# Moving the output LayerNorm of a two-layer graph-attention block from VectorE to GpSimd

## The chip, the cores and the metric

The kernel runs on one core of a Trainium2 chip. The metric is the device time of one execution in microseconds (us), the median of three. TensorE is called PE in the rows, VectorE DVE, ScalarE ACT, GpSimd POOL and SyncE SP.

## The reference

x has shape (8, 1024, 256), adj is a 1024 x 1024 matrix of zeros and ones. Two residual stages follow each other, each on the clipped LayerNorm of x. The first mixes nodes with adj, the second is graph attention with four heads, then one head, then a feed-forward part, and a last LayerNorm with gain and offset:

```python
h = relu(layernorm(x)); x = x + (deg * (h Wi + b) + adj @ (h Wj))      # stage 1
h = relu(layernorm(x))
# stage 2, for each batch b, layer 1 with 4 heads, layer 2 with 1 head:
e = f1[:, None] + f2[None, :]; e = where(e > 0, e, 0.01 * e); e = where(adj > 0, e, -1e9)
h' = elu(softmax(e) @ (h W))
y  = relu(h' @ w1 + b1) @ w2 + b2 + h'
mu = mean(y); var = var(y)
x  = x + (y - mu) / sqrt(var + 1e-5) * ln_gamma + ln_beta              # the part that the change touches
```

## The kernel before

After a setup block, one long block runs a software pipeline over "units". A unit is one 128-row tile of attention for one head: layer 1 has 32 units a batch (8 tiles x 4 heads), layer 2 has 8, so 320 units in all. Every engine's program is written as one loop over a step number n, and at step n each engine does the work of a few units at fixed distances, in a fixed order. At step n:

- VectorE makes the masked row of unit n+5 (`masked_row`, L935, which also gives its maximum `mx`), then the low half of the probabilities of unit n+1 (`low_part`, L942). Every second step it does the ELU of a pair (L950, L955) and, in layer 1, `ht_lo` (L961).
- GpSimd works on one column a row tile: `inverse` of unit n+2 (L736, L738: one over the sum of the exponentials, `rden`), and at even n `shifts` for units n+4 and n+5 (L749, L751: from `mx` to the exponent's shift).
- ScalarE makes the leaky ReLU of unit n+4 (L804), the exponential of unit n+3 (L810, which needs `shift`), then `high_part` of unit n+2 (L817, p_hi, which needs `rden` and frees nothing until `low_part` has read it).
- SyncE transposes p_hi and p_lo by DMA into four slots, which TensorE frees when it has multiplied a pair; TensorE does a pair every second step.

`masked_row` of a unit waits for `low_part` five units before it, since five row buffers `xr` are there.

Around this run the other jobs, placed by a step number relative to a batch: `front` (the first stage of a batch three ahead: LayerNorm L996, h0 L1002, the bias L1008, `cat_low` L1015, products L1156) and, relative to the end of layer 2 of batch s (`at = n - end2[s]`), the feed-forward part of batch s in two halves i of four row tiles each. Half i goes: at 4i the first product, at 1 + 4i ScalarE's `hidden` (L875), at 2 + 4i the second product, at 3 + 4i VectorE's `y_out` (L1048 adds b2, L1051 and L1058 give mean and variance of four tiles in `mv_y`), at 4 + 4i GpSimd's `rsqrt` (L722, L724: `rstd_y`), at 5 + 4i VectorE's `gain` (L1066), at 6 + 4i VectorE's `rescale` (L1075), and at 7 + 4i and 8 + 4i GpSimd adds two row tiles each to the output in memory (`add_y`, L759, a DMA with accumulation). Both halves share `mv_y` and `rstd_y`, so `y_out` of the next half waits, ahead of L1058, until the last readers of the half before are through.

For batches 0 to 5 all of this lies inside the attention of the next batches; for batch 6 beside the last eight units; for batch 7 after everything else.

Of the kernel before, what the change touches and what calls it, by code (L numbers as in the profile page):

```python
# [29 lines left out]
def build(nc, x, adj, w0, b0, w_heads, a_heads, w_out, a_out, w1, b1, w2, b2, gamma, beta, out):  # L30
# [12 lines left out]
    with ExitStack() as ctx:  # L43
# [530 lines left out]
        lny_stats, lny_mv, lny_eps, lny_pow, lny_gain, lny_done = (sem(f"lny_{i}") for i in ("stats", "mv", "eps", "pow", "gain", "done"))  # L574
# [144 lines left out]
        def _(pool):  # L719
# [33 lines left out]
            def add_y(p, i, u):  # L753

                pool.wait_ge(lny_done, 2 * p + i + 1)
                pool.wait_ge(x1_saved, 4 * (p + 1) * DMA)
                tok = slice((4 * i + 2 * u) * P, (4 * i + 2 * u + 2) * P)
                to = out[p:p + 1, tok, :].rearrange("b (t p) f -> p (b t) f", p=P)
                pool.dma_start(to, y_half[i][:, 2 * u * F:2 * (u + 1) * F].rearrange("p (t f) -> p t f", f=F), accum_op=ALU.add).then_inc(out_added[i], DMA)  # L759

# [5 lines left out]
            for n in range(START, STOP):  # L766
# [5 lines left out]
                for s in range(B):  # L772
# [11 lines left out]
                    for i in range(2):  # L784
                        if at == 4 + 4 * i:
                            pool.wait_ge(lny_mv, 2 * s + i + 1)
                            rsqrt(rstd_y[:, :], mv_y[:, :, 1], lny_eps, lny_pow, None, 2 * s + i + 1, T // 2)
                        for u in range(2):
# [133 lines left out]
        def _(dve):  # L922
# [119 lines left out]
            def y_out(p, i):  # L1042
# [11 lines left out]
                if 2 * p + i:  # L1054
                    hold(dve, "dve", lny_gain, 2 * p + i)
                    hold(dve, "dve", lny_pow, 2 * p + i)
# [3 lines left out]

            def gain(p, i):

                dve.wait_ge(lny_mv, 2 * p + i + 1)
                for t in range(half):
                    part = y_half[i][:, t * F:(t + 1) * F]
                    last = nc.vector.scalar_tensor_tensor(part, part, mv_y[:, t, 0:1], gamma_bc[:, :], ALU.subtract, ALU.mult)  # L1066
                last.then_inc(lny_gain, 1)

            def rescale(p, i):

                dve.wait_ge(lny_gain, 2 * p + i + 1)
                dve.wait_ge(lny_pow, 2 * p + i + 1)
                for t in range(half):
                    part = y_half[i][:, t * F:(t + 1) * F]
                    last = nc.vector.scalar_tensor_tensor(part, part, rstd_y[:, t:t + 1], beta_bc[:, :], ALU.mult, ALU.add)  # L1075
                last.then_inc(lny_done, 1)

            for n in range(START, STOP):
# [12 lines left out]
                for s in range(B):  # L1091
# [49 lines left out]
                    for i in range(2):  # L1141
                        if at == 3 + 4 * i:
                            y_out(s, i)
                        if at == 5 + 4 * i:
                            gain(s, i)
                        if at == 6 + 4 * i:
                            rescale(s, i)
# [195 lines left out]
```

## Time and profile before

| | us |
|---|---|
| median of 3 runs | 1901.22 (1899.51 to 1907.97) |
| the profiled execution | 1900.6 |
| its span, first to last instruction | 1898.8 |
| TensorE busy | 1656.0 (87%) |
| VectorE busy | 1472.8 (78%) |
| ScalarE busy | 1392.4 (73%) |
| GpSimd busy | 1027.7 (54%) |

The span covers all of the execution but 1.8 us. The busy shares are means over stretches of different kinds: no engine is full on average, and which one sets the pace changes along a batch. So the chain of waits and the order in time matter more than the shares.

### The profile page before, as it was taken

The numbers are of one execution on the slowest core, as the hardware profiler recorded it, in microseconds if no ns is written. First come the engines' busy times: TensorE is split into PE (matmuls) and PEld (weight loads), VectorE is DVE, ScalarE is ACT, GpSimd is POOL, SyncE is SP. The second block draws the span as 40 slices with busy tenths as digits, with TensorE's granted clock in tenths as the row PEclk, the third lists the DMA queues.
The fourth block names the chain that finished last, engine by engine and source line by source line (L and its number), as shares of the span: only waits on it lengthen the run. The fifth ranks groups of instructions, "written<-read, shape, count | busy, mean of one in ns | idle before, by whom it ended". The sixth has DMA issues, their size and how long they took to land.

```text
span 1898.8 us, 34621 instructions
## 1 busy us (share of the span) xinstructions
PE 1656.0 (87%) x12568; PEld 1277.1 (67%) x12568; DVE 1472.8 (78%) x2459; ACT 1392.4 (73%) x1789; POOL 1027.7 (54%) x1414
## 2 busy tenths in 40 slices
PE   6679888989989899898999899898998889987856
PEld 4448765777767777586676777676775776766644
DVE  6787877878797888877887787978788788787553
ACT  4088886869768797678867698687976798698550
POOL 2055563556465565655556564656556555576341
PEclk9799989999999899998999899998999999999988
DMA  6156793578756885677946887668846777688562
GB/s 216 39 117 103 126 179 66 99 110 161 132 96 107 129 177 94 101 97 138 172 89 108 113 167 127 95 112 126 180 90 107 92 140 145 108 136 126 95 95 40
DMA packets 713292, 225.57 MB, mean 119 GB/s; under 512 B 678784, under 2 KB 706432, under 8 KB 712992
## 3 DMA queue, kind: packets, MB, share of 16 engines
q1 hardware_dynamic: 704160, 214.92, 63.2%
q0 software_dynamic: 8960, 8.42, 3.8%
q8 instruction: 100, 1.64, 0.4%
q14 instruction: 72, 0.59, 0.1%
HBM read 38.54 MB, written 16.94 MB: 29 GB/s over the span
## 4 chain that ended last, share of the span: by engine, by line
PE 43%; DVE 18%; DMA 11%; ACT 9%; issue 9%; POOL 3%; SPq 2%; DVEq 0%; ACTq 0%; POOLq 0%
PE ps L1156 15%; DMA pt_hi<-p_hi 8%; PE ps L1184 7%; PE ps L1177 7%; PE ps L1178 7%; DVE p_lo L942 5%; DVE xr L935 4%; PE ps L1197 4%; ACT p_hi L817 2%; ACT xr L804 2%; PE ps L1276 2%; ACT xr L810 2%; ACT eq L823 1%; DVE stats_y L1051 1%; DVE val_lo L1039 1%
## 5 line engine op out<-in xcount | busy, mean ns | idle before, releaser
L1177 PE MATMUL ps<-pt_hi,val_hi 128*128 128x256 f16 x2048 | 471.2, 276 | 28.3 <-DVE eq L955 15.9
L817 ACT ACTIVATE p_hi<-xr,rden 128x1024 f16<-128x1024 f32 x320 | 365.3, 1142 | 164.3 <-POOL rden L738 91.9
L1178 PE MATMUL ps<-pt_hi,val_lo 128*128 128x256 f16 x2048 | 470.4, 276 | 0.0
L942 DVE SCALAR_TENSOR_TENSOR p_lo<-xr,rden,p_hi 128x1024 f16<-128x1024 f32 x320 | 409.9, 1282 | 17.2 <-ACT p_hi L817 17.1
L810 ACT ACTIVATE xr<-xr,shift 128x1024 f32<-128x1024 f32 x320 | 364.6, 1139 | 0.0
L736 POOL TENSOR_SCALAR den<-sums 128x1 f32<-128x1 f32 x320 | 142.0, 444 | 405.1 <-ACT xr L810 403.7
L749 POOL TENSOR_SCALAR zt<-mx,f1h 128x1 f32<-128x1 f32 x256 | 208.3, 813 | 243.5 <-DVE mx L935 240.5
L804 ACT ACTIVATE xr<-xr,f1h 128x1024 f32<-128x1024 f32 x256 | 292.6, 1143 | 63.8 <-DVE mx L935 62.7
L935 DVE CUSTOM_DVE_ANT_0 xr<-cat,mask_add 128x1024 f32<-128x1024 f32 x256 | 311.7, 1218 | 14.2 <-DMA cat<-f_rows 7.3
L738 POOL TENSOR_TENSOR rden<-den,minus_one 128x1 f32<-128x1 f32 x320 | 288.2, 901 | 26.6
L1184 PE MATMUL ps<-pt_lo,val_hi 128*128 128x256 f16 x2048 | 267.8, 274 | 4.0 <-DMA pt_lo<-p_lo 3.9
L1177 PEld LDWEIGHTS ps<-pt_hi,val_hi 128*128 128x128 f16 x2048 | 203.2, 99 | 66.0 <-DVE eq L955 23.0
L1197 PE MATMUL ps<-wo_hi,ht_hi 128*128 128x258 f16 x512 | 147.7, 288 | 95.9 <-DVE f12o L969 75.1
L751 POOL TENSOR_SCALAR shift<-zt 128x1 f32<-128x1 f32 x320 | 207.5, 648 | 31.7
L1178 PEld LDWEIGHTS ps<-pt_hi,val_lo 128*128 128x128 f16 x2048 | 203.1, 99 | 30.1 <-issue 2.6
L1184 PEld LDWEIGHTS ps<-pt_lo,val_hi 128*128 128x128 f16 x2048 | 201.2, 99 | 30.6 <-issue 6.2
L1197 PE MATMUL ps<-wo_hi,ht_lo 128*128 128x258 f16 x512 | 147.9, 289 | 0.0
L1197 PE MATMUL ps<-wo_lo,ht_hi 128*128 128x258 f16 x512 | 147.3, 288 | 0.0
L950 DVE TENSOR_SCALAR eq<-eq 128x512 f32<-128x512 f32 x160 | 68.5, 428 | 94.4 <-ACT eq L823 93.8
L967 DVE SCALAR_TENSOR_TENSOR valo_lo<-ps,valo_hi 128x512 f16<-128x512 f32 x32 | 22.1, 691 | 151.8 <-ACT valo_hi L836 151.8
L1197 PEld LDWEIGHTS ps<-wo_hi,ht_hi 128*128 128x128 f16 x512 | 51.9, 101 | 117.6 <-issue 77.4
L1177 PE MATMUL ps<-pt_hi,valo_hi 128*128 128x256 f16 x512 | 117.4, 276 | 12.7 <-DVE big L955 10.4
(185 smaller groups left out, 3260.8 us busy)
## 6 DMA issues: line engine op xcount, KB each, us to landing
cat<-f_rows SPq DMA_DIRECT2D x32, 512.0 KB, 4.8
out<-xx SPq DMA_DIRECT2D x32, 256.0 KB, 2.9
out<-big POOLq DMA_DIRECT2D x32, 256.0 KB, 5.2
xx<-in_x SPq DMA_DIRECT2D x28, 256.0 KB, 4.8
pt_hi<-p_hi SPq DMA_TRANSPOSE x320, 3.3
pt_lo<-p_lo SPq DMA_TRANSPOSE x320, 3.2
adj_i<-in_adj SPq DMA_DIRECT2D x4, 1024.0 KB, 10.8
f2o<-f2o_rows SPq DMA_DIRECT2D x8, 512.0 KB, 4.5
```

The lines of the kernel that those rows point to most:

```text
L738: nc.gpsimd.tensor_tensor(rden[:, c], den[:, c], minus_one[:, :], ALU.pow).then_inc(rden_done, 1)
L749: nc.gpsimd.tensor_scalar(zt[:, c], mx[:, c], -1.0, f1, ALU.mult, ALU.subtract).then_inc(shift_half, 1)
L804: nc.scalar.activation(line, line, ACT.Prelu, bias=f1, alpha=ALPHA).then_inc(r_done, 1)
L810: nc.scalar.activation(line, line, ACT.Exp, bias=shift[:, k % 8:k % 8 + 1], accum_out=sums[:, k % 8:k % 8 + 1]).then_inc(p_done, 1)
L817: nc.scalar.activation(p_hi[:, k % P_SLOTS, :], xr[:, k % X_SLOTS, :], ACT.Copy, scale=rden[:, k % 8:k % 8 + 1]).then_inc(hi_done, 1)
L935: nc.vector.tensor_tensor_reduce(out=xr[:, k % X_SLOTS, :], in0=cat[:, m, :] if layer == 1 else f2o[:, :], in1=mask_row[:, tile, :], scale ...
L942: nc.vector.scalar_tensor_tensor(p_lo[:, k % P_SLOTS, :], xr[:, k % X_SLOTS, :], rden[:, k % 8:k % 8 + 1], p_hi[:, k % P_SLOTS, :], ALU.mu ...
L1156: last = nc.tensor.matmul(to, lhsT, rhs, start=i == 0, stop=i == len(pairs) - 1)
L1177: nc.tensor.matmul(to, vh, hi, start=t == 0, stop=False)
L1178: nc.tensor.matmul(to, vl, hi, start=False, stop=False)
L1184: last = nc.tensor.matmul(to, vh, pt_lo[:, slot:slot + 2, t * P:(t + 1) * P], start=False, stop=t == T - 1)
L1197: last = nc.tensor.matmul(psD[:, u * 512:u * 512 + V], h[:, c % 2, ft, tok], w[:, KF * m + ft, :], start=m == 0 and ft == 0 and g == 0, st ...
```

## The change

The eight instructions a half that VectorE does in `gain` and `rescale` (one for each of four row tiles, twice) go away. GpSimd gets `normalise_y(p, i, t)`, three instructions a row tile, so twelve a half: subtract the mean and multiply by the inverse deviation, multiply by gamma, add beta. Two tiles are issued at step 5 + 4i and two at 6 + 4i, behind GpSimd's own work of that step. Each of the three waits for the one before. `add_y` waits for the tiles that it sends, and `y_out` of the next half waits for all four tiles of the half before.

```diff
             def add_y(p, i, u):
-                pool.wait_ge(lny_done, 2 * p + i + 1)
+                pool.wait_ge(lny_done, half * (2 * p + i) + 2 * u + 2)
...
+            def normalise_y(p, i, t):
+
+                part = y_half[i][:, t * F:(t + 1) * F]
+                count = half * (2 * p + i) + t + 1
+                if t == 0:
+                    pool.wait_ge(lny_pow, 2 * p + i + 1)
+                nc.gpsimd.tensor_scalar(part, part, mv_y[:, t, 0:1], rstd_y[:, t:t + 1], ALU.subtract, ALU.mult).then_inc(lny_unit, 1)
+                pool.wait_ge(lny_unit, count)
+                nc.gpsimd.tensor_tensor(part, part, gamma_bc[:, :], ALU.mult).then_inc(lny_gain, 1)
+                pool.wait_ge(lny_gain, count)
+                nc.gpsimd.tensor_tensor(part, part, beta_bc[:, :], ALU.add).then_inc(lny_done, 1)
...
+                        for t in range(half):
+                            if at == 5 + 4 * i + t // 2:
+                                normalise_y(s, i, t)
...
                 if 2 * p + i:
-                    hold(dve, "dve", lny_gain, 2 * p + i)
-                    hold(dve, "dve", lny_pow, 2 * p + i)
+                    hold(dve, "dve", lny_done, half * (2 * p + i))
...
-            def gain(p, i):
...
-                    last = nc.vector.scalar_tensor_tensor(part, part, mv_y[:, t, 0:1], gamma_bc[:, :], ALU.subtract, ALU.mult)
-            def rescale(p, i):
...
-                    last = nc.vector.scalar_tensor_tensor(part, part, rstd_y[:, t:t + 1], beta_bc[:, :], ALU.mult, ALU.add)
...
-                        if at == 5 + 4 * i:
-                            gain(s, i)
-                        if at == 6 + 4 * i:
-                            rescale(s, i)
```

GpSimd's program before, from `rsqrt` of a first half (steps 4 to 7): one inverse, one inverse, two pairs of shifts, one inverse, the DMA.

```order
L724 TENSOR_TENSOR rstd_y<-rstd_y,half_neg 128x4
L736 TENSOR_SCALAR den<-sums 128x1
L738 TENSOR_TENSOR rden<-den,minus_one 128x1
L736 TENSOR_SCALAR den<-sums 128x1
L738 TENSOR_TENSOR rden<-den,minus_one 128x1
L749 TENSOR_SCALAR zt<-mx,f1h 128x1
L751 TENSOR_SCALAR shift<-zt 128x1
L749 TENSOR_SCALAR zt<-mx,f1h 128x1
L751 TENSOR_SCALAR shift<-zt 128x1
L736 TENSOR_SCALAR den<-sums 128x1
L738 TENSOR_TENSOR rden<-den,minus_one 128x1
L759 DMA out<-big 128x2x256
```

The same engine and place after the change (`big` is the buffer in which the y tiles lie), beginning with the same first inverse:

```order
L736 TENSOR_SCALAR den<-sums 128x1
L738 TENSOR_TENSOR rden<-den,minus_one 128x1
L767 TENSOR_SCALAR big<-big,mv_y,rstd_y 128x256
L769 TENSOR_TENSOR big<-big,gamma_bc 128x256
L771 TENSOR_TENSOR big<-big,beta_bc 128x256
L767 TENSOR_SCALAR big<-big,mv_y,rstd_y 128x256
L769 TENSOR_TENSOR big<-big,gamma_bc 128x256
L771 TENSOR_TENSOR big<-big,beta_bc 128x256
L736 TENSOR_SCALAR den<-sums 128x1
L738 TENSOR_TENSOR rden<-den,minus_one 128x1
L749 TENSOR_SCALAR zt<-mx,f1h 128x1
L751 TENSOR_SCALAR shift<-zt 128x1
```

Six of the twelve new instructions stand between the first and the second inverse. The other six stand behind the second pair of shifts, ahead of the third inverse and the DMA. The same holds for the second half.

VectorE's program before at step 5, from `low_part` on, where `gain` stands (the row with ISA is the masked row):

```order
L942 SCALAR_TENSOR_TENSOR p_lo<-xr,rden,p_hi 128x1024
L1066 SCALAR_TENSOR_TENSOR big<-big,mv_y,gamma_bc 128x256 x4
L1002 SCALAR_TENSOR_TENSOR hs_lo<-yy,hs_hi 128x1024
L996 TENSOR_SCALAR yy<-xx,mv,rstd 128x256 x4
L935 ISA xr,mx<-cat,mask_add 128x1024
```

The same place after the change, with VectorE's lines moved by 15:

```order
L957 SCALAR_TENSOR_TENSOR p_lo<-xr,rden,p_hi 128x1024
L1017 SCALAR_TENSOR_TENSOR hs_lo<-yy,hs_hi 128x1024
L1011 TENSOR_SCALAR yy<-xx,mv,rstd 128x256 x4
L950 ISA xr,mx<-cat,mask_add 128x1024
L950 ISA mx 128x1
```

The four `gain` instructions have gone and nothing else has changed its place; `rescale` (L1075) goes in the same way one step later. Behind them comes `y_out` of the second half, whose L1058 now waits for GpSimd's last tile.

## Rows read from the trace of the kernel before

**Rows 1.** The page: busy time of the engines, and the chain by engine

```profile
PE 1656.0 (87%) x12568; PEld 1277.1 (67%) x12568; DVE 1472.8 (78%) x2459; ACT 1392.4 (73%) x1789; POOL 1027.7 (54%) x1414
...
PE 43%; DVE 18%; DMA 11%; ACT 9%; issue 9%; POOL 3%; SPq 2%; DVEq 0%; ACTq 0%; POOLq 0%
```

**Rows 2.** Chain of waits in batch 1's feed-forward stretch: start, us, what

```profile
753.06 1.58 DVE big L1066 x4
...
760.21 1.59 DVE big L1075 x4
...
769.72 3.25 DVE xx L1008 x8
...
774.22 1.26 POOL zt L749
...
778.43 1.94 POOL rstd_y L724
...
793.11 5.31 PE ps L1156 x16
```

**Rows 3.** GpSimd in order of time, 742 to 806 us: start, us, instruction

```profile
750.82 1.94 POOL L724 TENSOR_TENSOR rstd_y<-rstd_y,half_neg 128x4 f32<-128x4 f32 x1
...
753.87 0.47 POOL L736 TENSOR_SCALAR den<-sums 128x1 f32<-128x1 f32 x1
754.41 1.85 POOL L738 TENSOR_TENSOR rden<-den,minus_one 128x1 f32<-128x1 f32 x1
...
759.80 0.57 POOL L751 TENSOR_SCALAR shift<-zt 128x1 f32<-128x1 f32 x1
...
782.88 0.57 POOL L738 TENSOR_TENSOR rden<-den,minus_one 128x1 f32<-128x1 f32 x1
```

**Rows 4.** ScalarE in order of time, same stretch, idle before it in brackets

```profile
753.92 1.15 ACT L817 ACTIVATE p_hi<-xr,rden 128x1024 f16<-128x1024 f32 x1 [3.19 <-POOL rden L738]
...
786.47 1.13 ACT L817 ACTIVATE p_hi<-xr,rden 128x1024 f16<-128x1024 f32 x1
```

**Rows 5.** VectorE in order of time, same stretch

```profile
768.32 0.38 DVE L1058 BATCH_NORM_AGGREGATE mv_y<-stats_y 128x2 f32<-128x6 f32 x4 [0.37 <-DVE stats_y L1051]
...
790.64 1.28 DVE L942 SCALAR_TENSOR_TENSOR p_lo<-xr,rden,p_hi 128x1024 f16<-128x1024 f32 x1
791.84 1.22 DVE L1015 SCALAR_TENSOR_TENSOR big<-ps,big 128x1024 f16<-128x1024 f32 x1
```

**Rows 6.** Groups of GpSimd's instructions: busy us and mean ns, idle before

```profile
L738 POOL TENSOR_TENSOR rden<-den,minus_one 128x1 f32<-128x1 f32 x320 | 288.2, 901 | 26.6
L749 POOL TENSOR_SCALAR zt<-mx,f1h 128x1 f32<-128x1 f32 x256 | 208.3, 813 | 243.5 <-DVE mx L935 240.5
...
L346 POOL TENSOR_TENSOR sq<-whf 128x2048 f32<-128x2048 f32 x1 | 3.6, 3600 | 4.1 <-DMA wof<-in_L_gnn_W_out 4.1
...
L343 POOL TENSOR_TENSOR sq<-w_sb 128x1024 f32<-128x1024 f32 x1 | 1.9, 1892 | 5.4 <-DMA w_sb<-in_L_gnn_W 5.4
```

**Rows 7.** One line each of GpSimd: duration ns min/median/max

```profile
L738 POOL TENSOR_TENSOR rden<-den,minus_one x320: 567/568/1854, 111.0 to 1840.6; 128x1 f32<-128x1 f32 x160
...
L749 POOL TENSOR_SCALAR zt<-mx,f1h x256: 285/694/2137, 100.1 to 1734.4; 128x1 f32<-128x1 f32 x128
```

**Rows 8.** Setup in order of time, VectorE beside a long GpSimd instruction

```profile
27.72 3.60 POOL L347 TENSOR_TENSOR sqo<-wof 128x2048 f32<-128x2048 f32 x1
...
29.17 0.14 DVE L421 TENSOR_SCALAR eb<-kf 128x1 f32<-128x1 f32 x1
29.35 1.99 DVE L422 TENSOR_SCALAR e<-eb 128x2 int32<-128x2 f32 x1
```

**Rows 9.** Who waited for whom, SyncE's queue: us in total, times, longest

```profile
SPq L699 <- PE ps L1184: 224.2, 77, 7.6
```

**Rows 10.** Chain of waits at the end of batch 6: start, us, what

```profile
1842.31 0.82 POOL out L759
1843.12 6.40 DMA out<-big
1849.62 0.76 DVE big L955
```

**Rows 11.** GpSimd in order of time, from 1836 us on

```profile
1837.03 0.24 POOL L736 TENSOR_SCALAR den<-sums 128x1 f32<-128x1 f32 x1
...
1888.49 1.14 POOL L724 TENSOR_TENSOR rstd_y<-rstd_y,half_neg 128x4 f32<-128x4 f32 x1
1891.71 2.54 POOL L759 DMA_DIRECT2D out<-big  x2 [2.08 <-DVE big L1075]
```

More of the change, by code:

```diff
@@ L573, in build @@
         ln1_stats, ln1_mv, ln1_eps, ln1_pow, ln1_rstd, ln1_yn = (sem(f"ln1_{i}") for i in ("stats", "mv", "eps", "pow", "rstd", "yn"))
-        lny_stats, lny_mv, lny_eps, lny_pow, lny_gain, lny_done = (sem(f"lny_{i}") for i in ("stats", "mv", "eps", "pow", "gain", "done"))
+        lny_stats, lny_mv, lny_eps, lny_pow, lny_unit, lny_gain, lny_done = (sem(f"lny_{i}") for i in ("stats", "mv", "eps", "pow", "unit", "gain", "done"))
         h0hi_half, h0_half, h1hi_half, h1_half = sem("h0hi_half"), sem("h0_half"), sem("h1hi_half"), sem("h1_half")
@@ L1059, in y_out @@
                 last.then_inc(lny_mv, 1)
-            def gain(p, i):
-                dve.wait_ge(lny_mv, 2 * p + i + 1)
-                for t in range(half):
-                    part = y_half[i][:, t * F:(t + 1) * F]
-                    last = nc.vector.scalar_tensor_tensor(part, part, mv_y[:, t, 0:1], gamma_bc[:, :], ALU.subtract, ALU.mult)
-                last.then_inc(lny_gain, 1)
-            def rescale(p, i):
[L1071 to L1074, printed above, removed]
-                    last = nc.vector.scalar_tensor_tensor(part, part, rstd_y[:, t:t + 1], beta_bc[:, :], ALU.mult, ALU.add)
-                last.then_inc(lny_done, 1)
             for n in range(START, STOP):
```

## Prediction

> **What bounds the kernel now.** The page comes first. TensorE is busy 87% of the span, VectorE 78%, GpSimd only 54%, and the chain that ended last is 43% TensorE, 18% VectorE and 3% GpSimd [rows 1]. That invites one to hand VectorE's work to GpSimd. A share says nothing of where the work lies, so the chain in order of time is next, over one batch. Batches 0 to 5 each have their feed-forward stretch inside the attention of later batches, and I read batch 1's. There the chain leaves TensorE for some 50 us: it runs over VectorE, and both groups of instructions that the change removes are on it, 1.58 and 1.59 us, in the first half. At 769.72 VectorE is still the chain, from 774.22 GpSimd is (`zt`, then the power for `rstd_y`), and at 793.11 TensorE takes over again [rows 2]. So in this stretch VectorE is really short of time, and GpSimd is too: for all its idle time elsewhere, ScalarE waits 3.19 us for its `rden` at 753.92 [rows 4].
>
> Third, GpSimd in order of time. The power ends at 752.76, one inverse follows, and from 753.87 to 760.37 come the second inverse and four shift instructions, 6.50 us for six instructions with one column each [rows 3]. Such an instruction can be short (`rden` 567 ns, `zt` 285 ns [rows 7]) but takes 901 and 813 ns in the mean [rows 6]. They stretch while VectorE runs: `rden` at 754.41 took 1.85 us. In setup the block goes the other way: a VectorE instruction on two columns, both operands in the on-chip memory, took 1.99 us at 29.35 and ended at 31.34, just when GpSimd's 3.60 us product from 27.72 ended, while its neighbour on one column took 0.14 us [rows 8]. So the two engines shut each other out for whole instructions.
>
> **The change, part by part.** *Removed from VectorE:* 128 instructions, eight a half. On the chain they are 1.58 + 1.59 = 3.2 us in each first half; those of the second half are not on it [rows 2].
>
> *Added to GpSimd:* twelve a half, six in each of two steps. The trace has no 128x256 instruction of this engine. Two-input products took 1892 ns at 1024 columns and 3600 ns at 2048 [rows 6], so 1.67 ns a column and 0.18 us fixed: 0.61 us at 256. The one-input instruction lies between the shortest `zt`, 0.29 us, and 0.61 us; I take 0.5. Between dependent ones about 0.09 us pass (753.87 + 0.47 to 754.41 is 0.07 [rows 3]). A tile is then 0.5 + 0.61 + 0.61 + 3 x 0.09 = 2.0 us, and the six of a step 4.0 us bare. On top comes the wait for VectorE's instructions. Over the run it is 901 - 567 = 0.33 us for `rden` and 813 - 285 = 0.53 for `zt` [rows 6, 7], and about 0.7 in the six instructions of this stretch. I take 0.5 us, so N = 4.0 + 6 x 0.5 = 7.0 us for a step's six (6.0 to 8.2 by those bounds).
>
> *Where it lands, first half.* `y_out` of the second half needs the last tile of the first before its L1058, which ran at 768.32 [rows 5]. GpSimd is there at 753.87 + N + 6.50 + N = 760.4 + 2N. Bare, 2 x 4.0 gives 768.4: no wait, and none of the 3.2 us is kept either. With N = 7.0 it is 774.4. But VectorE comes to the wait at about 768 (3.2 us earlier by what was removed, some 3 us later by being shut out by eight or nine of the new instructions, a third of a microsecond each, about half of their own length, since only part of VectorE's instructions here have two on-chip operands) and then stands still, which leaves GpSimd alone, so its last six take some 4.6: 772.0. That is +3.7 us, and behind the wait stand h0, the bias, and the next masked row, from which the chain runs to GpSimd's `zt` [rows 2]. The bounds are 0 and, if each instruction cost a microsecond more than bare, 753.9 + 10 + 6.5 + 8 = 778.4, so +10.
>
> *Second half.* Six new instructions come before the inverse that ended at 783.45 [rows 3] and that ScalarE used at 786.47 [rows 4]: slack 3.0. With N = 7.0 it is ready at 783.45 + 3.7 + 7.0 = 794.2, and p_hi of that unit ends 1.15 us later, at 795.3, where `low_part` stood at 790.64 [rows 5]: +4.7, thus 1.0 of its own over the 3.7. `cat_low` (L1015) stands behind it and starts the product with which TensorE takes over. The other six delay the next inverse by some 10 us. This I cost at nothing, for the cover is large: SyncE's transposes waited 224.2 us in 77 places for TensorE to free a slot [rows 9], so after this stretch the softmax runs ahead of TensorE. If that cover were gone, it would be 4 us more. Together 4.7 us a batch, and 6 x 4.7 = 28.
>
> *Batch 6.* The chain at its end is GpSimd's output DMA at 1842.31, its landing 6.40 us later, then VectorE at 1849.62 [rows 10]. Now the order is: from 1837.03 an inverse (0.9), six new ones bare (4.0), an inverse (0.9), six (4.0), an inverse (0.9), the DMA: 1847.7 [rows 11]. That is +5.4, and about +1 for its first half.
>
> *Batch 7.* Nothing hides it. Before, two thirds of a microsecond after the power VectorE's `rescale` was under way, and the DMA went out at 1891.71 [rows 11]. Now eight microseconds of GpSimd (4 x 2.0) stand between the power's end, 1889.63, and the DMA. The first half's twelve and its two DMA issues (2.5 us) also make the second half's power start 1.8 us late. 1889.63 + 1.8 + 8.0 + 0.2 = 1899.6, so +7.9.
>
> *Sum:* 28 + 1 + 5.4 + 7.9 = 42. The profiled execution took 1900.6 us, 0.6 under the median of the runs; 1901.2 + 42 = 1943, and I say 1943.
>
> The Trainium skill (SBUF — State Buffer, section "SBUF: two separate sides") says that VectorE and GpSimd share a pair of ports by an exclusive lock: whichever of a two-input or two-port VectorE instruction and a GpSimd instruction starts first keeps the other out until it ends. The trace agrees, with the 1.99 us above. By this rule alone, with every wait the rest of a 1.28 us VectorE instruction, the mean wait would be 0.64 and N 7.8, and the sum 6 us more than mine. The skill's GPSIMD Engine Reference, section 3.1, gives 4497 ns for a two-input addition of 2048 columns; the trace shows 3600 ns for a product. By the page each of the eight two-input instructions of a half would be 0.15 us longer, some 7 us over the sum; the trace decides.
>
> **The rivals.** *B, GpSimd is worse than I cost it.* If 256-column instructions wait for more than the one VectorE instruction in flight, a microsecond each, the first half is +10 and the second +4: 14 a batch, 84 + 14 = 98, so 1999. For it speaks that the longest `zt` took 2.14 us [rows 7]; against it, that VectorE stands still once it waits. It decides from a mean wait of 0.8 us on. *C, hidden but for the ends.* If the contention were near nothing, 760.4 + 2 x 4.0 = 768.4 makes the first half even, and only batches 6 and 7 pay: 1901.2 + 14 = 1915. Against it is the stretch's mean of 0.7 us. *D, VectorE's relief is kept.* 3.2 us saved in six batches, minus 14: 1901.2 - 19 + 14 = 1896, within half a per cent. It needs 2N below 4.7, so six instructions in 2.4 us, well under bare. *E, faster.* VectorE is the engine that is short, and all eight instructions a half count, 6.4 us a batch: 1901 - 38 + 14 = 1877. For it speaks that VectorE is the chain for most of 742 to 774; it needs D's condition and as much in the second half, where `gain` and `rescale` are not on the chain. That the change does nothing is excluded by batch 7 alone.
>
> **How the numbers follow.** My forecast (per batch 2 to 8 us) gets 0.52, B 0.24, C 0.13, D 0.07, E 0.04. What measurement of this kernel can tell from no change is about 0.5%, 9.5 us, so 1891.7 to 1910.7. C lies mostly above that, its lower third inside: same 0.04 + 0.07 = 0.11, faster 0.04, slower 0.85. The range reaches from C's lower part, 1908, to the middle of B, 1985.
>
> **What would show it.** In the profile after: the new one-input and two-input lines at 1.0 to 1.3 us in the mean against 0.5 and 0.61 in batch 7; VectorE's L1058 (now L1072) waiting for GpSimd's last tile in every batch, 3 to 4 us each; ScalarE's wait for `rden`, 3.19 and more here, grown; VectorE's own masked rows and `low_part` with a longest value of about 0.6 us over the usual; TensorE's clock granted lower in that stretch; 8 us between the last power and the last DMA. Wrong it would be if the wait at L1058 is not there, or if `low_part` in the second half is no later than before, or if TensorE is kept waiting some 100 us further on, where I cost the late inverses at nothing.

## The result and the profile after

The changed kernel takes 1981.27 us, the median of 4 runs (1980.34 to 1983.99), against 1902.1 for the kernel before in the same comparison: a ratio of 1.0414 (95% interval 1.0387 to 1.0441). It is 79 us slower, where the prediction said 42. The profiled execution has a span of 1978.8 us, 80.0 more than before.

The page of the changed kernel, busy times and the chain by engine, as in [rows 1]:

```profile
PE 1664.3 (84%) x12568; PEld 1278.6 (65%) x12568; DVE 1441.8 (73%) x2331; ACT 1394.5 (70%) x1789; POOL 1210.2 (61%) x1606
...
PE 40%; POOL 18%; DVE 12%; DMA 8%; issue 8%; ACT 8%; SPq 1%; DVEq 0%; ACTq 0%; POOLq 0%
```

VectorE is 31 us less busy and GpSimd 182 us more, but GpSimd's 61% is still the lowest share of the five. Its share of the chain went from 3% to 18%. The share says that GpSimd has room, the chain that it is what the end waits for.

**Where the 80 us arise.** The first power of each batch's feed-forward part (L724) is a good mark, since it occurs once a batch. Its start moved by 0, 8.0, 16.2, 22.7, 30.7 and 39.2 us in batches 0 to 5: batches 0 to 4 cost 6.5 to 8.4 each, 7.8 in the mean. The last three marks, batches 5, 6 and 7, before the change:

```profile
1632.88 1.95 POOL L724 TENSOR_TENSOR rstd_y<-rstd_y,half_neg 128x4 f32<-128x4 f32 x1
...
1813.65 1.12 POOL L724 TENSOR_TENSOR rstd_y<-rstd_y,half_neg 128x4 f32<-128x4 f32 x1
...
1877.88 1.13 POOL L724 TENSOR_TENSOR rstd_y<-rstd_y,half_neg 128x4 f32<-128x4 f32 x1
```

After the change the same three marks, GpSimd in order of time, then batch 7 from its first power:

```profile
1672.05 1.94 POOL L724 TENSOR_TENSOR rstd_y<-rstd_y,half_neg 128x4 f32<-128x4 f32 x1
...
1867.17 1.05 POOL L724 TENSOR_TENSOR rstd_y<-rstd_y,half_neg 128x4 f32<-128x4 f32 x1
...
1943.89 1.05 POOL L724 TENSOR_TENSOR rstd_y<-rstd_y,half_neg 128x4 f32<-128x4 f32 x1
1945.05 1.24 POOL L767 TENSOR_SCALAR big<-big,mv_y,rstd_y 128x256 f32<-128x256 f32 x1
1946.37 0.73 POOL L769 TENSOR_TENSOR big<-big,gamma_bc 128x256 f32<-128x256 f32 x1
1947.18 0.73 POOL L771 TENSOR_TENSOR big<-big,beta_bc 128x256 f32<-128x256 f32 x1
...
1956.31 2.52 POOL L759 DMA_DIRECT2D out<-big  x2
...
1959.20 1.05 POOL L724 TENSOR_TENSOR rstd_y<-rstd_y,half_neg 128x4 f32<-128x4 f32 x1
...
1971.58 2.54 POOL L759 DMA_DIRECT2D out<-big  x2
```

The shifts are 39.2, 53.5 and 66.0 us at the marks, and 79.9 at the last DMA (1971.58 against 1891.71 [rows 11]). So batch 5 cost 14.3, batch 6 12.5 and batch 7 13.9. Batch 7 shows the new instructions bare, with VectorE idle: 1.24 us for the one-input instruction and 0.73 for each two-input one. From the power's end to the DMA 11.3 us pass, where 8.0 were forecast.

**The stretch of batch 1.** Busy time of each engine, from a product of TensorE to the same product behind the stretch; before the change:

```profile
core 0: us, PE busy (x) PEld busy (x) DVE busy (x) ACT busy (x) POOL busy (x), PEclk, DMA share, GB/s
733.70:809.20 75.50, 68.42 (x490) 51.12 (x488) 61.75 (x108) 52.02 (x68) 47.77 (x61) 0.95 0.62 97
```

and after it:

```profile
741.80:825.30 83.50, 68.62 (x490) 50.71 (x488) 58.30 (x92) 52.39 (x68) 70.08 (x83) 0.94 0.53 86
```

GpSimd was busy in 47.8 of 75.5 us and is now in 70.1 of 83.5; TensorE, ScalarE and the clock hardly changed. The chain of waits after the change in that stretch, which answers to [rows 2]:

```profile
756.51 1.52 POOL zt L749
...
758.84 1.94 POOL rstd_y L724
...
762.69 1.35 POOL big L767
...
772.81 1.25 POOL big L767
...
793.28 0.57 POOL rden L738
...
800.20 0.72 POOL big L771
...
801.23 0.58 POOL rden L738
...
804.78 1.61 DVE xr L950
...
806.40 1.66 DVE p_lo L957
808.06 1.15 DVE big L1030
...
809.25 5.26 PE ps L1149 x16
```

From 756.51 to 801.81 every piece is GpSimd's, but for gaps of about 0.1 us. Where VectorE was the chain before, GpSimd is now. TensorE takes over at 809.25 instead of 793.11, 16.1 later, of which 8.0 come from batch 0.

VectorE in that stretch, in order of time (idle before an instruction in brackets), beside [rows 5]:

```profile
773.12 0.50 DVE L965 TENSOR_SCALAR eq<-eq 128x512 f32<-128x512 f32 x1 [5.40 <-ACT eq L838]
...
780.57 0.38 DVE L1072 BATCH_NORM_AGGREGATE mv_y<-stats_y 128x2 f32<-128x6 f32 x4 [0.26 <-POOL big L771]
```

The wait that the prediction named, L1072 for GpSimd's last tile, is 0.26 us, here and in the second halves of all batches 0 to 5. In the first halves of batches 1 to 5, where no tile is waited for, VectorE stands 0.26 us before it as well. VectorE comes to it late, since it has already waited 5.40 us for the exponential of the ELU (L838). That one stands on ScalarE behind p_hi, and p_hi waits for `rden`, which stands behind six new instructions. Over the whole run, who waited for whom (us in total, times, longest), the changed kernel:

```profile
ACT p_hi L832 <- POOL rden L738: 212.3, 65, 6.1
DVE eq L965 <- ACT eq L838: 177.1, 64, 8.6
...
DVE p_lo L957 <- ACT p_hi L832: 47.5, 20, 5.5
```

and before:

```profile
DVE eq L950 <- ACT eq L823: 93.8, 57, 8.6
ACT p_hi L817 <- POOL rden L738: 91.9, 38, 6.5
...
DVE p_lo L942 <- ACT p_hi L817: 17.1, 11, 3.3
```

### The profile page after: what moved, and what is told of

It is laid out like the page before. It is cut to its first block, busy times and chain, and to the rows that moved or that the text cites. A ratio compares the mean times of both kernels' runs of the same rounds, so it can differ in the third digit from the quotient of the medians.

```text
span 1978.8 us, 34654 instructions
## 1 busy us (share of the span) xinstructions
PE 1664.3 (84%) x12568; PEld 1278.6 (65%) x12568; DVE 1441.8 (73%) x2331; ACT 1394.5 (70%) x1789; POOL 1210.2 (61%) x1606
## 4 chain that ended last, share of the span: by engine, by line
PE 40%; POOL 18%; DVE 12%; DMA 8%; issue 8%; ACT 8%; SPq 1%; DVEq 0%; ACTq 0%; POOLq 0%
PE ps L1149 15%; PE ps L1170 6%; PE ps L1177 6%; DMA pt_hi<-p_hi 6%; PE ps L1171 6%; POOL big L767 4%; PE ps L1190 4%; DVE p_lo L957 3%; DVE xr L950 3%; POOL big L771 3%; POOL big L769 3%; ACT p_hi L832 2%; ACT xr L819 2%; POOL rden L738 2%; ACT xr L825 2%
## 5 line engine op out<-in xcount | busy, mean ns | idle before, releaser
L832 ACT ACTIVATE p_hi<-xr,rden 128x1024 f16<-128x1024 f32 x320 | 365.5, 1142 | 285.3 <-POOL rden L738 212.3
L957 DVE SCALAR_TENSOR_TENSOR p_lo<-xr,rden,p_hi 128x1024 f16<-128x1024 f32 x320 | 417.4, 1305 | 52.7 <-ACT p_hi L832 47.5
L736 POOL TENSOR_SCALAR den<-sums 128x1 f32<-128x1 f32 x320 | 149.8, 468 | 352.0 <-ACT xr L825 350.6
L950 DVE CUSTOM_DVE_ANT_0 xr<-cat,mask_add 128x1024 f32<-128x1024 f32 x256 | 316.3, 1235 | 17.6 <-DMA cat<-f_rows 9.4
L749 POOL TENSOR_SCALAR zt<-mx,f1h 128x1 f32<-128x1 f32 x256 | 193.4, 755 | 201.6 <-DVE mx L950 198.4
L738 POOL TENSOR_TENSOR rden<-den,minus_one 128x1 f32<-128x1 f32 x320 | 275.2, 860 | 26.7
L1171 PEld LDWEIGHTS ps<-pt_hi,val_lo 128*128 128x128 f16 x2048 | 203.7, 99 | 30.8 <-issue 3.4
L751 POOL TENSOR_SCALAR shift<-zt 128x1 f32<-128x1 f32 x320 | 194.5, 608 | 31.6
L965 DVE TENSOR_SCALAR eq<-eq 128x512 f32<-128x512 f32 x160 | 68.7, 430 | 177.7 <-ACT eq L838 177.1
L1149 PE MATMUL ps<-adjT,hs_hi 128*128 128x512 f16 x224 | 93.2, 416 | 51.3 <-DVE big L1030 39.7
```

What stands on the lines that cost most here:

```text
L738: nc.gpsimd.tensor_tensor(rden[:, c], den[:, c], minus_one[:, :], ALU.pow).then_inc(rden_done, 1)
L751: nc.gpsimd.tensor_scalar(shift[:, c], zt[:, c], ALPHA, zt[:, c], ALU.mult, ALU.min).then_inc(shift_done, 1)
L832: nc.scalar.activation(p_hi[:, k % P_SLOTS, :], xr[:, k % X_SLOTS, :], ACT.Copy, scale=rden[:, k % 8:k % 8 + 1]).then_inc(hi_done, 1)
L950: nc.vector.tensor_tensor_reduce(out=xr[:, k % X_SLOTS, :], in0=cat[:, m, :] if layer == 1 else f2o[:, :], in1=mask_row[:, tile, :], scale ...
L957: nc.vector.scalar_tensor_tensor(p_lo[:, k % P_SLOTS, :], xr[:, k % X_SLOTS, :], rden[:, k % 8:k % 8 + 1], p_hi[:, k % P_SLOTS, :], ALU.mu ...
L1149: last = nc.tensor.matmul(to, lhsT, rhs, start=i == 0, stop=i == len(pairs) - 1)
```

## The experiments

Four theories were set against each other. **Queue and port:** GpSimd does one thing at a time, and where its stretch is full, each microsecond added to it lengthens the run. **The wait:** the shared `mv_y`, as the prediction had it. **Bursts:** not the amount but six instructions at a time hold up the small columns. **Relief:** how much VectorE's lost work gives back. Ratios are to the kernel before beside each run. That kernel took between 1900 and 1909 us beside the different runs, so times of different comparisons are set against each other by their ratios. Spans are those of one profiled execution each, and good to some 5 us. Where a sum over the run is given for the added instructions, it is the three groups' busy time.

### 1. relief_only: neither engine normalises

`gain` and `rescale` are gone and nothing is put in their place, so the rows go out without normalisation, gain and offset.

```diff
-                pool.wait_ge(lny_done, 2 * p + i + 1)
+                pool.wait_ge(lny_pow, 2 * p + i + 1)
...
-                        if at == 5 + 4 * i:
-                            gain(s, i)
-                        if at == 6 + 4 * i:
-                            rescale(s, i)
```

> Leaves out the normalisation of the output rows altogether: neither VectorE nor GpSimd subtracts the mean, scales, or applies gamma and beta; rows are added to the output as they are. This prices what VectorE's eight instructions a half were worth. Theory A (only the first halves' two groups lie on the chain, 3.2 us in each of six batches, and about 2 us at the very end): about 1880 us. Rival (all eight instructions of both halves count, 6.4 us a batch): about 1860. Rival (nothing is gained, GpSimd's columns are what the stretch waits for): 1899.

1888.8 us, ratio 0.9918 (0.9887 to 0.9948), a span of 1884.1. VectorE is 52 us less busy than before and the run only 15 us shorter, nearest to theory A. With GpSimd's work as it was, the relief is worth some 15 us, so what was added to GpSimd costs some 95 us in the change.

### 2. load_only: GpSimd's twelve instructions added, VectorE's work kept

The kernel before, with the same three instructions a tile on a spare row (`y_out` adds beta in place of b2, whose row is the spare one). Nothing waits for them but what stands behind them in GpSimd's queue.

```diff
+                nc.gpsimd.tensor_scalar(extra[:, :], extra[:, :], sc[:, 9:10], sc[:, 10:11], ALU.subtract, ALU.mult).then_inc(extra_0, 1)
+                pool.wait_ge(extra_0, count)
+                nc.gpsimd.tensor_tensor(extra[:, :], extra[:, :], gamma_bc[:, :], ALU.mult).then_inc(extra_1, 1)
+                pool.wait_ge(extra_1, count)
+                nc.gpsimd.tensor_tensor(extra[:, :], extra[:, :], beta_bc[:, :], ALU.add).then_inc(extra_2, 1)
```

> The kernel before, VectorE's gain and rescale in place, and GpSimd given the same twelve instructions a half at the same steps, on a scratch row that nobody waits for. The scratch row is the one that held b2, so y gets beta added in place of b2. If the price is GpSimd's queue (the inverses stand behind the new instructions) and VectorE being shut out, the time is about 1975 or more, since VectorE's own work is still there, less some 12 us for batch 7's tail, which no longer waits: 1970. If the price is mainly the waits on the new results (the mean and variance of the second half behind the last tile of the first, the output DMA behind the tiles), it is about 1925.

2004.89 us, ratio 1.0531 (1.0498 to 1.0564), a span of 2003.9: 105 over before. The groups of the new instructions (busy us, mean ns of one | idle before):

```profile
L768 POOL TENSOR_SCALAR b_bc<-b_bc,sc 128x256 f32<-128x256 f32 x64 | 112.5, 1757 | 3.8
L772 POOL TENSOR_TENSOR b_bc<-b_bc,beta_bc 128x256 f32<-128x256 f32 x64 | 64.9, 1014 | 5.0
L770 POOL TENSOR_TENSOR b_bc<-b_bc,gamma_bc 128x256 f32<-128x256 f32 x64 | 60.7, 949 | 5.3
```

They are busy for 238 us. No data waits for them, and the loss is larger than the change's. So the price is paid in the queue, not in the waits that the change writes down. It is also some 30 us more than the 1970 to 1975 that I had written for this case. In a loaded run VectorE's relief is worth some 105 - 80 = 25 us, more than the 15 of relief_only. I had expected the end of the run to be spared, and it was not: the output DMA stands behind them in GpSimd's queue.

### 3. last_on_vector: batch 7 as before, the others as after

```diff
+        def on_vector(p, i):
+            return p >= B - 1
...
-                            if at == 5 + 4 * i + t // 2:
+                            if at == 5 + 4 * i + t // 2 and not on_vector(s, i):
```

> The changed kernel, but for batch 7 VectorE normalises as before. If the end is a plain serial term, the distance from the power's end to the DMA twice in batch 7, then 13 to 14 us come back: about 1968. If part of the end was already caused earlier, less: 1974 or more.

1968.96 us, ratio 1.0332 (1.0298 to 1.0366), 12 us under the change, as expected. In its trace 12.8 us lie between the first power of batch 7 (1952.41) and the last DMA (1965.19), where the change has 27.7 and the kernel before 13.8.

### 4. immediates: the one-input instruction with two constants

The rows are not normalised: a constant takes the place of each row's mean and inverse deviation.

```diff
-                nc.gpsimd.tensor_scalar(part, part, mv_y[:, t, 0:1], rstd_y[:, t:t + 1], ALU.subtract, ALU.mult).then_inc(lny_unit, 1)
+                nc.gpsimd.tensor_scalar(part, part, 0.25, 1.5, ALU.subtract, ALU.mult).then_inc(lny_unit, 1)
```

> The changed kernel, with the one-input instruction of GpSimd given two constants in place of the two columns (mean and inverse deviation), so the rows are not normalised: 0.25 is subtracted and the result multiplied by 1.5. If the two column operands make it 1.22 us, it falls to 0.6 or less in batch 7, and the time by 5 us there and some 3 us in each other batch: about 1955. If its length is that of any two-step one-input instruction on 256 columns, it stays at 1.22 and the time at 1981.

1974.17 us, ratio 1.0363 (1.0335 to 1.039), 7 us less by the medians and 10 by the ratios, and so between the two forecasts. One line of the trace of immediates (duration in ns, min/median/max):

```profile
L767 POOL TENSOR_SCALAR big<-big x64: 1063/1134/2136, 532.4 to 1962.0; 128x256 f32<-128x256 f32 x64
```

Of the bare 1.22 us only 0.15 are the two column operands. The rest is the length of this kind of instruction on 256 columns.

### 5 and 6. two_stats and spread: the named wait, and the burst

two_stats gives `mv_y` and `rstd_y` a second set, so `y_out` no longer waits for the half before. spread has this too, and one tile a step over four steps instead of two tiles over two.

```diff
-        den = sb("den", [P, 8], F32)
+        den = sums
...
-        mv_y = sb("mv_y", [P, T // 2, 2], F32)
+        mv_y = sb("mv_y", [P, 2, T // 2, 2], F32)
...
-                            if at == 5 + 4 * i + t // 2:
+                            if at == 5 + 4 * i + t:
```

(The last pair is spread's alone.)

> The changed kernel with mean, variance and inverse deviation kept in a set for each half, so that the second half's mean and variance no longer wait for the first half's last tile. (den shares its eight columns with sums, for room.) The trace after has that wait at 7.9 us in total over 8 places. If it is worth its 7.9 us, 1973. If the inverses behind the new instructions carry the first half's price anyway, it gives back next to nothing: 1979 to 1981. If it was the main price, as the prediction had it (3.7 us in each of six batches), 1959 or less.

1984.39 us, ratio 1.0415 (1.0397 to 1.0432): nothing gained. The wait on which the prediction's first term was built costs nothing by itself.

> As two_stats, and GpSimd does one row tile a step over four steps (5 to 8 of the first half, 9 to 12 of the second) in place of two tiles in two steps. If the price is how long an inverse or a shift stands behind new instructions, a step's 7.5 us become 3.8 and half of the batches' price goes: about 1945. If it is GpSimd's total work in the stretch, or VectorE being shut out as often as before, it stays within 10 us of two_stats: about 1970.

1982.28 us, ratio 1.0412 (1.0391 to 1.0434): nothing gained either, where the theory of bursts said 1945. The theory of bursts fell. ScalarE waits 196.3 us for `rden` in 82 places instead of 212.3 in 65: the same work, in smaller pieces.

### 7. pow_load: the same time in GpSimd's queue, hardly any in memory

Like load_only, and with its effect on `b2`, but the instructions are powers on 5, 2 and 2 columns, bare 1.16, 0.70 and 0.69 us.

```diff
+                nc.gpsimd.tensor_tensor(extra[:, 0:5], sc[:, 9:14], half_neg[:, 0:5], ALU.pow).then_inc(extra_0, 1)
+                pool.wait_ge(extra_0, count)
+                nc.gpsimd.tensor_tensor(extra[:, 0:2], sc[:, 9:11], half_neg[:, 0:2], ALU.pow).then_inc(extra_1, 1)
+                pool.wait_ge(extra_1, count)
+                nc.gpsimd.tensor_tensor(extra[:, 0:2], sc[:, 9:11], half_neg[:, 0:2], ALU.pow).then_inc(extra_2, 1)
```

> As load_only (VectorE as in the kernel before, y gets beta in place of b2, nobody waits for GpSimd's extra results), but the three instructions of a tile are powers on 5, 2 and 2 columns, which by the trace's 0.57 us for one column and 1.05 for four last about as long by themselves (1.2, 0.7, 0.7 us) and read and write almost nothing. It separates the time in GpSimd's queue from the port that it shares with VectorE. Queue alone: near load_only's 2005, at least 1990. If shutting each other out is half of the price or more: 1955 or less.

1965.2 us, ratio 1.0322 (1.0307 to 1.0336), a span of 1963.4: 65 over before, against load_only's 105. VectorE's `low_part`, duration in ns (min/median/max), in pow_load:

```profile
L958 DVE SCALAR_TENSOR_TENSOR p_lo<-xr,rden,p_hi x320: 1273/1279/1300, 113.6 to 1903.4; 128x1024 f16<-128x1024 f32 x160
```

and in load_only:

```profile
L958 DVE SCALAR_TENSOR_TENSOR p_lo<-xr,rden,p_hi x320: 1272/1280/1739, 113.3 to 1940.9; 128x1024 f16<-128x1024 f32 x160
```

The result lies between the two forecasts, 1990 and more or 1955 and less. The powers never stretch VectorE's instruction, the wide ones do. The powers themselves came to 199 us (1397, 826 and 884 ns in the mean), so they waited less, but they did wait. Some 60% of load_only's cost is time in GpSimd's queue, these waits included. The remaining 40 us are close to the 39 us by which the added GpSimd time differs (238 - 199). Some 8 of those are shorter instructions (2.54 us a tile bare against 2.66, 64 tiles); the rest comes with the wide operands.

The Trainium skill (SBUF — State Buffer, section "SBUF: two separate sides") has the mechanism: an exclusive lock on a shared pair of ports, kept for a whole instruction. For the wide instructions the trace agrees in kind: `low_part` takes up to 1.74 us beside them. It does not for the powers: each lasts 0.7 to 1.2 us by itself, and beside 192 of them no `low_part` took more than 1.30.

### 8. later_on_vector: VectorE keeps the work, at other steps

The kernel before, with two sets as in 5; `gain` and `rescale` of batches 0 to 5 come 4 steps later in the first half and 1 later in the second.

```diff
+        def late(s, i):
+            return (4, 1)[i] if s < B - 2 else 0
...
-                        if at == 5 + 4 * i:
+                        if at == 5 + 4 * i + late(s, i):
                             gain(s, i)
-                        if at == 6 + 4 * i:
+                        if at == 6 + 4 * i + late(s, i):
                             rescale(s, i)
```

> The kernel before, with VectorE still normalising, but in batches 0 to 5 the first half's gain and rescale stand four steps later (9 and 10) and the second half's one step later (10 and 11), the output DMAs with them, and a set of mean and deviation for each half (den shares its columns with sums). If VectorE is what the first half waits for, 2 to 3 us a batch come back, as relief_only had 11 us by the end of batch 4: about 1890. If the same work is only paid a few steps further on: 1900.

1906.96 us (11 runs), ratio 1.0012 (1.0000 to 1.0024): no gain. In its trace the second power of a batch follows the first 1.9 to 3.3 us sooner than before in batches 0 to 5, but the next batch's first power is no earlier, so the work is paid a few steps further on. Moving the eight instructions on VectorE's own queue does not win what their place on the chain [rows 2] promised.

### 9 and 10. unit_only and first_halves: how much room GpSimd has, and where

unit_only leaves gamma and beta out (only the first instruction a tile is done). first_halves does the whole work, first halves on GpSimd and second halves on VectorE.

```diff
-                nc.gpsimd.tensor_scalar(part, part, mv_y[:, t, 0:1], rstd_y[:, t:t + 1], ALU.subtract, ALU.mult).then_inc(lny_unit, 1)
-                pool.wait_ge(lny_unit, count)
-                nc.gpsimd.tensor_tensor(part, part, gamma_bc[:, :], ALU.mult).then_inc(lny_gain, 1)
-                pool.wait_ge(lny_gain, count)
-                nc.gpsimd.tensor_tensor(part, part, beta_bc[:, :], ALU.add).then_inc(lny_done, 1)
+                nc.gpsimd.tensor_scalar(part, part, mv_y[:, t, 0:1], rstd_y[:, t:t + 1], ALU.subtract, ALU.mult).then_inc(lny_done, 1)
```

```diff
+        def on_vector(p, i):
+            return i == 1
```

> The changed kernel with only the first of GpSimd's three instructions a tile; gamma and beta are left out, so the output lacks the gain and the offset of the last LayerNorm. It adds some 90 us of GpSimd time in place of 223. Theory (GpSimd has about 140 us of room beside the pipeline, and only what is over it counts, about one for one, as 199, 214, 223 and 238 us of added time gave): the middle batches lose nothing, the ends a few us, and VectorE's relief is still there: 1890 to 1905. Rival (each microsecond added ahead of an inverse counts in the same share, 80/223): 1901 + 90 x 0.36 = 1933.

1903.06 us (10 runs), ratio 1.0018 (1.0007 to 1.0029), and the group of its added instruction:

```profile
L767 POOL TENSOR_SCALAR big<-big,mv_y,rstd_y 128x256 f32<-128x256 f32 x64 | 100.1, 1569 | 0.2
```

100 us more on GpSimd, 6.3 a half, and less than 0.3% on the run. That is not for nothing, since VectorE's relief is in it: relief_only, with the same relief and no added work, has a span of 1884.1, unit_only one of 1899.4. The 100 us cost some 15, about 1 us a half. At the first power of batch 5 they are 7: it comes 11.2 us earlier than in the kernel before in relief_only and 4.5 earlier in unit_only. At the change's price, 95 us for 223, they would have cost 43. So the price is not proportional to the work.

> GpSimd normalises the first halves, VectorE the second ones, at their old steps: 112 us of added GpSimd time. By the room theory: 1895 to 1910, since 112 is under 140, less half of VectorE's relief. By the chain of the changed kernel, in which the first half alone delays the masked row behind it by 4.1 us a batch in batches 0 to 4, and more in 5 and 6: 5 x 4 + 13 and 2 in batch 7, 1936.

1934.47 us, ratio 1.0186 (1.017 to 1.0201), as the chain of the changed kernel said (1936). GpSimd's added time is 112 us, little more than the 100 of unit_only, yet the run is 34 us longer. VectorE keeps half of its work here, which by relief_only is at most 15 us of that. For the rest the two runs differ in how the work lies: 6 us in every half against 14 in each first half. The room is local to a half; what one half leaves unused is no room for the other.

### 11 and 12. exp_first and exp_first_before: the ELU's exponential ahead of p_hi

The road of the loss in batch 1 went over ScalarE: `rden`, p_hi, the exponential behind it, VectorE. Both runs let the exponential go first, exp_first in the changed kernel and exp_first_before in the kernel before.

```diff
-                if unit_at(n + 2) is not None:
-                    high_part(unit_at(n + 2))
                 if pair_at(n - 4) is not None:
                     elu_exp(pair_at(n - 4))
+                if unit_at(n + 2) is not None:
+                    high_part(unit_at(n + 2))
```

> The changed kernel, with ScalarE's exponential for the ELU of a pair ahead of that step's p_hi instead of behind it. In the trace of the changed kernel VectorE stands 5.40 us in front of the ELU at 773, since the exponential stands behind a p_hi that waits for GpSimd's late inverse, and so do the masked row and all of y_out behind it. If that is the road on which the late inverses reach the chain, some 3 to 5 us of each batch's 8 and half of batch 5's 13 come back: 1950. If the late inverses reach it by p_hi and low_part themselves anyway: 1978.

1978.72 us, ratio 1.0364 (1.034 to 1.0388), as the second forecast said and not the 1950 of the first. By the medians it is 3 us under the change, by the ratios 0.5%, so at most some 10 us of the 30 came back. Who waited for whom in exp_first:

```profile
ACT p_hi L832 <- POOL rden L738: 225.2, 80, 5.8
...
DVE p_lo L957 <- ACT p_hi L832: 101.0, 36, 6.3
...
DVE eq L965 <- ACT eq L838: 76.2, 57, 8.6
...
DVE mv_y L1072 <- POOL big L771: 24.5, 8, 3.3
```

The wait for the exponential fell from 177.1 to 76.2. `low_part`'s wait for p_hi doubled (47.5 to 101.0), and L1072's wait for GpSimd grew from 7.9 to 24.5. Take one road away and the next carries most of the loss. What all of them have in common is GpSimd's queue.

> The kernel before with the same exchange on ScalarE, to see what the exchange does without the change. There ScalarE waited 91.9 us for inverses and VectorE 93.8 us for this exponential. If the exchange is neutral where GpSimd is not late: 1897 to 1902. If p_hi's 0.7 us delay every second step lengthens the softmax's round more than it helps: 1915.

1891.52 us, ratio 0.9912 (0.9889 to 0.9935) to the 1909.26 beside it. This version is 0.9% faster than the kernel before by exchanging two calls, with VectorE keeping the normalisation. Beside it exp_first takes 87 us more (1978.72 to 1891.52), so with the exchange in both kernels the change costs no less than without. That it gains through the shorter wait for the exponential (61.6 against 93.8 us in the kernel before) is argued, not shown.

## Why the prediction was right in sign and half the size

**What holds: direction, queue, port.** The added work, not a new dependence, is the price. Where GpSimd has room it costs little (unit_only, 100 us of work for some 15). Where it has none, the run grows. The result lies near the upper end of the range that was given (1908 to 1985). With all twelve instructions a half, the added time in GpSimd and the lengthening of the span are:

| | added on GpSimd | VectorE relieved | span longer |
|---|---|---|---|
| pow_load | 199 us | no | 65 us |
| load_only | 238 us | no | 105 us |
| immediates | 214 us | yes | 73 us |
| after | 223 us | yes | 80 us |

39 us more on GpSimd cost 40 (the first two rows), 9 more cost 7 (the last two). The first pair has the wide operands in it and the second is hardly more than the scatter of single spans, so that a microsecond beyond the room costs about one is suggested, not shown. From unit_only to the change 123 us more on GpSimd cost 79.

**Removed from VectorE (3.2 us a first half).** Six batches with 3.2 are 19 us; relief_only gave 15 in the whole run, load_only against the change some 25. The sum kept nothing of it. That error has the other sign, so the cost of the added work was missed by more than the 38 us that the total is off.

**N = 7.0 for six instructions.** Near: 7.8 (762.64 to 770.43) and 7.5 us (772.79 to 780.33) in batch 1. That is luck, since two errors offset each other. Six bare ones took 5.7 us and not 4.0 (batch 7, 11.3 for twelve): the one-input term was 1.22 us and not 0.5, the two-input one 0.72 and not 0.61. The trace's products from which 0.61 was worked out square one tile (`sq<-whf`), so both inputs were the same. The prediction set aside the figure of the Trainium skill (GPSIMD Engine Reference, section 3.1). Its estimate by that figure, 0.15 us more, so 0.76, was nearer to the 0.72. The wait for VectorE was 0.29, 0.25 and 0.28 us in the mean (1508, 976 and 1005 ns over the bare 1.22 and 0.72), and neither 0.5 nor the 0.64 worked out from the lock.

The groups of the new instructions in the changed kernel:

```profile
L767 POOL TENSOR_SCALAR big<-big,mv_y,rstd_y 128x256 f32<-128x256 f32 x64 | 96.5, 1508 | 0.2
L771 POOL TENSOR_TENSOR big<-big,beta_bc 128x256 f32<-128x256 f32 x64 | 64.3, 1005 | 5.0
L769 POOL TENSOR_TENSOR big<-big,gamma_bc 128x256 f32<-128x256 f32 x64 | 62.5, 976 | 5.3
```

**First half, +3.7, by L1058's wait for the last tile.** The size is nearly right, the mechanism not. VectorE's masked row behind the second half's `y_out` starts at 772.89 before and 785.14 after: 12.2 later, 8.0 of it from batch 0, so +4.2. But the wait (now L1072) is 0.26 us there and 7.9 us in all 8 places of the run, and taking it away changed nothing (two_stats). The same slots of GpSimd delay VectorE by the other road first, p_hi and the exponential. The prediction looked for one wait that decides. There were three roads of near equal length out of one full queue. That the size came out all the same is luck too.

**Second half, +1.0.** This step failed, though the inverse that it followed and its time were right. That inverse, behind the first six new instructions of the second half, was forecast ready at 794.2, so at 802.2 with the 8.0 from batch 0. It was ready at 801.80, and p_hi started at 801.83. The error comes behind p_hi. The prediction let `low_part` follow the end of p_hi at once, 1.15 us from its start. But on ScalarE the exponential of the ELU stands behind p_hi, and VectorE does the ELU and the masked row ahead of `low_part`. VectorE before the change:

```profile
788.21 0.59 DVE L950 TENSOR_SCALAR eq<-eq 128x512 f32<-128x512 f32 x1 [0.85 <-ACT eq L823]
...
789.50 1.22 DVE L935 CUSTOM_DVE_ANT_0 xr<-cat,mask_add 128x1024 f32<-128x1024 f32 x1
```

and after it:

```profile
803.59 0.49 DVE L965 TENSOR_SCALAR eq<-eq 128x512 f32<-128x512 f32 x1 [6.10 <-ACT eq L838]
...
804.78 1.61 DVE L950 CUSTOM_DVE_ANT_0 xr<-cat,mask_add 128x1024 f32<-128x1024 f32 x1
...
806.33 1.73 DVE L957 SCALAR_TENSOR_TENSOR p_lo<-xr,rden,p_hi 128x1024 f16<-128x1024 f32 x1
807.98 1.21 DVE L1030 SCALAR_TENSOR_TENSOR big<-ps,big 128x1024 f16<-128x1024 f32 x1
```

From the start of p_hi to `low_part` 4.17 us passed before (786.47 [rows 4] to 790.64 [rows 5]) and 4.50 after, not 1.15. So the slack was 3.0 us, and the prediction used it twice: once ahead of p_hi and once more between p_hi's end and `low_part`. `cat_low` moved from 791.84 [rows 5] to 807.98, 16.1 us: 8.0 from batch 0, 4.2 from the first half, so 3.9 of its own. In batches 0 to 4 this own part is 3.6 to 3.9, and a batch costs 7.8 in the mean, not 4.7.

**The late third inverse at nothing.** It held in batches 0 to 4: TensorE's shift grew by 0.7 us at most behind the stretch. The starts of its product behind `cat_low` are 7.8, 16.1, 24.3, 30.8 and 38.5 us late in batches 0 to 4, and the next powers 8.0, 16.2, 22.7, 30.7 and 39.2.

**Batch 5 like the others (4.7).** It failed, by 9.6: 14.3 us. Batch 5 has no first stage of a later batch beside it, and no `cat_low` behind which TensorE takes over. The traces bear out that GpSimd was nearer to being the bound there: before the change the chain is GpSimd's for 22 of the 58 us from `y_out` of the first half to TensorE (1625.7 to 1684.0), in batch 1 for 8 of 51. The late third inverse, costed at nothing, is on the chain here: it started at 1664.28 before and starts at 1720.13 after, 55.9 later, of which the batch brought 39.2, and the chain goes through it. No run took batch 5 by itself, so how much of the 9.6 is this inverse stays open.

**Batch 6, +5.4 and +1.** 12.5 us. The chain at its end is GpSimd's and the DMA's as forecast: the DMA is issued at 1909.17 (1842.31 before [rows 10]). From the first power to the second 3.6 us more pass than before (22.3 to 25.9), where 1 was forecast, and from the second to the DMA 9.7 more (6.3 to 16.1), where 5.4 were. Four one-input instructions at 0.7 us each are 2.9 of those 4.3 missing. Behind the DMA 0.8 us come back.

**Batch 7, +7.9.** 13.9, and this is mostly the one-input term. Four bare tiles take 11.3 us and not 8.0, 2.9 of the difference by the one-input instruction, and both halves pay it: 2 x 3.3 = 6.6 over the forecast, 6.0 found. last_on_vector takes these microseconds away again.

So of the 38 us missing, 16 are batches 0 to 4 (5 x 3.1, nearly all in the second halves), 10 batch 5, and 12 batches 6 and 7, mostly the one-input instruction.

**The rivals.** B needed a mean wait of 0.8 us; it was 0.27, and a batch cost 7.8 and not 14. C had the first six batches pay nothing; they pay 53 of the 80 us. D and E needed six new instructions in 2.4 us, and they take 5.7 bare.

**The signs named in advance.** The new lines' means are 0.98 to 1.51 us, bare 0.72 and 1.22. ScalarE's wait for `rden` grew from 91.9 to 212.3. The clock fell little (0.95 to 0.94 in the stretch). `low_part`'s longest is 1.74, before 1.31, and the masked row's 1.63, before 1.24: 0.4 longer, where 0.6 was said. The wait at L1072 is nearly absent, and the prediction named that itself as what would show it wrong.

VectorE lost some of its relief in this way. One line of the changed kernel:

```profile
L957 DVE SCALAR_TENSOR_TENSOR p_lo<-xr,rden,p_hi x320: 1272/1281/1743, 114.0 to 1917.3; 128x1024 f16<-128x1024 f32 x160
```

In the mean `low_part` went from 1282 to 1305 ns. Times 320 that is 7 us. The engine's busy time fell by 31 us in the change, where it fell by 52 in relief_only.

## What to carry to other kernels

An engine's idle share is no room: ask how much it is idle in the very steps where the work will stand, and count what small, urgent instructions stand behind it in its queue. Here GpSimd, with 46% idle, took some 6 us a half for about 1 us each, and the next 8 a half for about 5. Follow a late result to its reader in the order of that engine's program: between p_hi and `low_part` stood the ELU and the masked row, and that was most of the miss in five batches. Neighbours in the trace are no bound for an instruction form that it lacks: the two-operation instruction on 256 columns came out at 1.22 us, where 0.29 and 0.61 had been taken as its bounds. And when several roads lead out of one full queue, removing one wait moves the loss to the next, as in exp_first; two_stats and spread gained nothing either.

## What the runs showed of the hardware

- On GpSimd, an instruction with one tensor input and two operations on 128x256 took 1.22 us bare, 1.07 with constants, and a two-input one 0.72. The Trainium skill (GPSIMD Engine Reference, section 4.1) calls one-input work about line-rate and two-input work twice as slow as VectorE's; for this form the measurement shows the opposite order. The second half of it agrees, 0.72 us against 1.58 for four of VectorE's [rows 2], though VectorE's do two operations each.
- Powers on GpSimd are long for their size: 0.57 us on one column, 0.70 on two, 1.16 on five.
- The lockout works both ways and can be told from the queue: the wide instructions stretched VectorE's (1.28 to 1.74 us), the powers on few columns did not (1.30 at most). `low_part` was lengthened by 0.46 us at most, less than the 0.72 to 1.22 us that the wide instructions last. By the comparison with pow_load some 30 of load_only's 105 us go with it.
